# One expert per tile of sorted tokens instead of all experts for every token

## The reference, cut to what matters

```
gate_logits = jnp.einsum('bpd,de->bpe', x, W_gate)
top_w, top_idx = jax.lax.top_k(gate_logits, K)            # K = 2 of E = 8
top_w = jax.nn.softmax(top_w, axis=-1)
...
for e in range(E):
    h = jax.nn.gelu(jnp.einsum('bpd,dm->bpm', x, W_in[e]) + b_in[e], approximate=False)
    y = jnp.einsum('bpm,md->bpd', h, W_out[e]) + b_out[e]
    out = out + combine[..., e, None] * y                 # combine is 0 for 6 of 8 experts
```

## Time and profile before

| | |
|---|---|
| median of 3 runs | 4415.43 us |
| the profiled execution, its own time | 4414.62 us |
| its span in the trace | 4412.8 us |
| busy share of the span | PE 94%, DVE 83%, ACT 74%, POOL 41% |
| expert phase, from its first instruction to the end | 3872.3 to 4412.8 us |

### The profile page before, as it was taken

How to read it: one execution, slowest core, us unless ns; L and a number is a source line. 1 busy time by engine, 2 the same in 40 slices (tenths; PEclk the granted TensorE clock), 3 DMA queues, 4 the chain that set the end, 5 groups by cost and what they waited for, 6 DMA issues and landing times. The chain is left out here.

```text
span 4412.8 us, 116370 instructions
## 1 busy us (share of the span) xinstructions
PE 4161.9 (94%) x43493; PEld 3278.8 (74%) x43493; DVE 3681.6 (83%) x6452; ACT 3261.0 (74%) x5155; POOL 1825.8 (41%) x983
## 2 busy tenths in 40 slices
PE   6887689999999999999999999999999999879999
PEld 2434268888888888888888888888888888757776
DVE  7889688888888888888888888888888888657776
ACT  5888567777777777777777777777777777546666
POOL 0000255555555555555555555555555555200000
PEclk9999799999999999999999999999999999979999
DMA  2111132322332323323233222333223222211110
GB/s 84 44 44 44 35 71 67 70 67 66 88 73 65 71 62 89 74 63 71 62 92 71 67 67 63 96 67 70 63 64 98 65 69 68 50 63 45 48 43 29
DMA packets 351688, 287.85 MB, mean 65 GB/s; under 512 B 231920, under 2 KB 236400, under 8 KB 350000
## 3 DMA queue, kind: packets, MB, share of 16 engines
q1 hardware_dynamic: 351152, 280.60, 26.1%
HBM read 45.45 MB, written 4.33 MB: 11 GB/s over the span
## 5 line engine op out<-in xcount | busy, mean ns | idle before, releaser
L702 POOL TENSOR_TENSOR qk_rotated<-qk_rotated,rotary_sines 128x1024 f32<-128x1024 f32 x384 | 924.3, 2407 | 1414.4 <-DVE rotary_sines L783 1414.4
L713 POOL TENSOR_TENSOR qk_rotated<-qk_rotated,rnorm 128x1024 f32<-128x1024 f32 x384 | 733.2, 1910 | 7.4
L791 DVE TENSOR_REDUCE qk_sumsq<-qk_squared 128x16 f32<-128x1024 f32 x384 | 465.3, 1212 | 97.5 <-ACT qk_squared L525 97.5
L232 PE MATMUL ps_proj<-qkv_w_hi,x_shifted_hi 128*128 128x512 f32 x1152 | 511.6, 444 | 15.9 <-DVE rotary_sines L783 11.7
L532 ACT ACTIVATE q_t<-ps_qk_t 128x512 f32<-128x512 f32 x384 | 229.5, 598 | 401.6 <-PE ps_qk_t L288 392.3
L773 DVE TENSOR_TENSOR qk_rotated<-ps_proj,rotary_scaled 128x1024 f32<-128x1024 f32 x384 | 467.2, 1217 | 7.6 <-ACT qk_squared L525 7.6
L783 DVE TENSOR_TENSOR rotary_sines<-ps_proj,rotary_scaled 128x1024 f32<-128x1024 f32 x384 | 466.3, 1214 | 1.7 <-POOL qk_rotated L702 1.7
L234 PE MATMUL ps_proj<-qkv_w_hi,x_shifted_lo 128*128 128x512 f32 x1152 | 459.6, 399 | 0.0
L546 ACT ACTIVATE k_t_by_head<-ps_qk_t 64x512 f32<-64x512 f32 x768 | 451.2, 587 | 11.0 <-PE ps_qk_t L297 1.6
L233 PE MATMUL ps_proj<-qkv_w_lo,x_shifted_hi 128*128 128x512 f32 x1152 | 456.1, 396 | 0.0
L313 PE MATMUL ps_scores<-k_t_by_head,q_t 128*32 128x128 f32 x12288 | 415.1, 276 | 9.8 <-ACT ps_scores L555 5.1
(11 more groups left out here) (304 smaller groups left out, 9694.7 us busy)
## 6 DMA issues: line engine op xcount, KB each, us to landing
v_by_window<-v_tokens SPq DMA_DIRECT2D x1152, 128.0 KB, 2.4
v_by_window<-v_tokens SPq DMA_DIRECT2D x384, 64.0 KB, 2.1
k_t_by_head<-k_t_by_head SPq DMA_DIRECT2D x96, 256.0 KB, 4.4
e_w_in<-combine_saved SPq DMA_DIRECT2D x64, 256.0 KB, 3.0
v_by_window<-v_by_window SPq DMA_DIRECT2D x192, 64.0 KB, 2.0
qkv_w_raw<-in_layer_qk_dram SPq DMA_DIRECT2D x7, 1664.0 KB, 8.8
f_k_stacked<-f_k_hi SPq DMA_DIRECT2D x64, 64.0 KB, 2.0
f_k_stacked<-f_k_lo SPq DMA_DIRECT2D x64, 64.0 KB, 2.0
```

The source lines that it names most:

```text
L232: mm(out, hi, HI[:, o:o + 512], start=True, stop=False)
L702: tt(u, u, TB[:], ALU.add).then_inc(added, 1)
L713: tt(u, u, r.unsqueeze(3).broadcast_to((P, 2, 8, DH)), ALU.mult).then_inc(scaled, 1)
L791: nc.vector.reduce_sum(SS[:, 16 * i:16 * i + 16], SQ[:].rearrange("p (h e) -> p h e", e=DH), AX).then_inc(sumsq, 1)
```

## The change

The dense loop over blocks and experts is replaced. First, for all 8 blocks: the sum x1, its layer norm, the normed rows turned to token order (`XR`, 130 words a row: 128 features, a destination and a weight) and back, the gate, and the top 2 of 8. A scan over all one-hot choices and two matmuls rank the 8192 choices by expert; each expert's run of slots is rounded up to a multiple of 512, so that there are at most 23 tiles (TILES) of 512 slots, and each tile has one expert. POOL then issues 64 indirect row transfers of 128 rows into a DRAM array `expert_rows`, which SP has filled with empty slots before (6.1 MB). Beside that runs the attention of all blocks, in an order of its own for each engine, and leaves the stream in `XF` (`base`). SP, ACT and POOL also split each expert's weights into high and low parts and store them in DRAM (1 MB an expert).

Then the tiles run, always 23. For tile t, SP loads 512 rows (266 KB, four buffers) and, by a register that it loads from `EID`, the bias and the split weights of the tile's expert (0.5 MB for each of the two matrices, two buffers). PE turns the rows, computes four hidden and four output quarters (each three split matmuls) and turns the result back; DVE weighs it; POOL writes its 512 rows to DRAM (`expert_y`) with four indirect transfers, by the destinations that came with the rows. At the end SP loads the two results of each token, DVE adds them to the stream, and SP stores it.

In the features phase the semaphores are cleared and given back at the end, with one more barrier, so that there are enough of them.

```diff
@@ features_phase @@
-            return ctx.enter_context(nc.semaphore("f_" + name))
+            signals.append(nc.alloc_semaphore(name="f_" + name))
+            return signals[-1]
...
+    nc.clear_and_free_semaphores(signals)
+    nc.all_engine_barrier()
...
@@ constants @@
+TILES = (TOPK * B * N + E_ * (BLK - 1)) // BLK
+NSLOT = TILES * BLK
+ROWW = P + 2
-HS_ = 3
+EHALF = 2 * HM * P
...
@@ experts_phase: sync @@
-            sp.dma_start(WI[:], w_in).then_inc(experts_in, 16)
-            sp.dma_start(WO[:], w_out).then_inc(experts_in, 16)
...
+            sp.dma_start(XN[:, 1:4, :], x_attn[:, 1:4, :]).then_inc(xa_in[0], 16)
+            sp.dma_start(XN[:, 4:NBLK, :], x_attn[:, 4:NBLK, :]).then_inc(xa_in[1], 16)
+            sp.dma_start(xs, slots).then_inc(filled, 16)
+            for e in range(2):
+                sp.dma_start(WR[e][:], expert_w[e]).then_inc(w_in[e], 16)
+            for e in range(E_):
+                sp.wait_ge(w_high, e + 1)
+                sp.wait_ge(w_low, e + 1)
+                sp.dma_start(split[e], WB[e % 2][:].rearrange("p s x -> p (s x)").bitcast(F32)).then_inc(w_saved[e % 2], 16)
+                if e + 2 < E_:
+                    sp.dma_start(WR[e % 2][:], expert_w[e + 2]).then_inc(w_in[e % 2], 16)
+            for k in range(2):
+                sp.wait_ge(w_saved[k], 16 * E_ // 2)
+            sp.wait_ge(expert_ids, 1)
+
+            def load_rows(t):
+
+                if t >= 4:
+                    sp.wait_ge(y_saved[t % 2], 16 * NT * ((t - 4) // 2 + 1))
+                if t >= 2:
+                    sp.wait_ge(x_hi, t - 1)
+                sp.dma_start(XT[t % 4][:].rearrange("p c d -> p (c d)"),
+                             xs[t * BLK:(t + 1) * BLK, :].rearrange("(p c) d -> p (c d)", c=NT)).then_inc(xt_in[t % 2], 16)
+
+            def load_weights(t):
+
+                e = sp.value_load(EID[0:1, t:t + 1], min_val=0, max_val=E_ - 1)
+                if t >= 2:
+                    sp.wait_ge(h_out, HM * (t - 1))
+                sp.dma_start(EB[t % 4][:], expert_b[e]).then_inc(wi_in[t % 2], 16)
+                sp.dma_start(WB[t % 2][:, 0, :].bitcast(F32), split[e, :, 0:EHALF]).then_inc(wi_in[t % 2], 16)
+                if t >= 2:
+                    sp.wait_ge(y_out, t - 1)
+                sp.dma_start(WB[t % 2][:, 1, :].bitcast(F32), split[e, :, EHALF:2 * EHALF]).then_inc(wo_in[t % 2], 16)
+            load_weights(0)
+            sp.wait_ge(scattered, 16 * NPOS)
+            load_rows(0)
+            for t in range(TILES):
+                if t + 1 < TILES:
+                    load_rows(t + 1)
+                if t > 0:
+                    load_weights(t)
+            for k in range(2):
+                sp.wait_ge(y_saved[k], 16 * NT * ((TILES + 1 - k) // 2))
+            for k in range(4):
+                w = 2 * NT * TOPK * P
+                sp.dma_start(YL[:, 2 * k:2 * k + 2].rearrange("p i c s d -> p (i c s d)"), ytok[:, k * w:(k + 1) * w]).then_inc(y_in[k], 16)
+            for i in range(NBLK):
+                sp.wait_ge(summed, i + 1)
+                sp.dma_start(out[:, i], tokens(XF2(XF, i))).then_inc(x_out, 16)
...
@@ experts_phase: tensor @@
+            def ranks():
+                pe.wait_ge(counted, 1)
+                mm(TOTAL[:, 0:E_], ONES[:], INC[:, :, NPOS - 1], start=True, stop=True).then_inc(rank_mm, 1)
+                pe.wait_ge(counted, 2)
+                pe.wait_ge(zc_out, NBLK)
+                mm(RANK[:], TRI[:], OH[:].rearrange("p e k -> p (e k)"), start=True, stop=False)
+                mm(RANK[:], ONES[:], EX[:].rearrange("p e k -> p (e k)"), start=False, stop=True).then_inc(rank_mm, 1)
...
+            def rows_in(t):
+                pe.wait_ge(xt_in[t % 2], 16 * (t // 2 + 1))
+                after(pe, x_hi, t)
+                after(pe, x_lo, t)
+                pe.wait_ge(base, NBLK)
+                for c in range(NT):
+                    last = flip(XP[:, chunk(c)], XT[t % 4][:, c, 0:P], IDENT[:])
+                last.then_inc(xp_mm, 1)
+
+            def hidden(t, m):
+                b = t % 2
+                if m == 0:
+                    pe.wait_ge(wi_in[b], 32 * (t // 2 + 1))
+                    pe.wait_ge(x_hi, t + 1)
+                after(pe, h_out, HM * (t - 1) + m + 1)
+                if t == 0:
+                    pe.wait_ge(hs_out, NBLK)
+                mm(HB[m][:], WB[b][:, 0, chunk(m)], XHI[b][:], start=True, stop=False)
+                mm(HB[m][:], WB[b][:, 0, chunk(HM + m)], XHI[b][:], start=False, stop=False)
+                if m == 0:
+                    pe.wait_ge(x_lo, t + 1)
+                mm(HB[m][:], WB[b][:, 0, chunk(m)], XLO[b][:], start=False, stop=True).then_inc(h_mm, 1)
+
+            def output(t, m):
+                b = t % 2
+                if m == 0:
+                    pe.wait_ge(wo_in[b], 16 * (t // 2 + 1))
+                    after(pe, y_out, t - 1)
+                pe.wait_ge(h_lo, HM * t + m + 1)
+                mm(YB[b][:], WB[b][:, 1, chunk(m)], HHI[:, b, m, :], start=(m == 0), stop=False)
+                mm(YB[b][:], WB[b][:, 1, chunk(m)], HLO[:, b, m, :], start=False, stop=False)
+                last = mm(YB[b][:], WB[b][:, 1, chunk(HM + m)], HHI[:, b, m, :], start=False, stop=(m == HM - 1))
+                if m == HM - 1:
+                    last.then_inc(y_mm, 1)
+
+            def rows_out(t):
+                pe.wait_ge(y_out, t + 1)
+                after(pe, yo_out, t)
+                for c in range(NT):
+                    last = flip(YT[:, chunk(c)], YS[t % 2][:, chunk(c)], IDENT[:])
+                last.then_inc(yt_mm, 1)
+            rows_in(0)
+            for t in range(TILES + 2):
+                for m in range(HM):
+                    if t < TILES:
+                        hidden(t, m)
+                    if 0 <= t - 1 < TILES:
+                        output(t - 1, m)
+                    if m == 1 and t + 1 < TILES:
+                        rows_in(t + 1)
+                    if m == 2 and t >= 2:
+                        rows_out(t - 2)
...
@@ experts_phase: scalar @@
+            def weights_high(e):
+                b = e % 2
+                act.wait_ge(w_in[b], 16 * (e // 2 + 1))
+                after(act, w_saved[b], 16 * (e // 2))
+                a(WB[b][:, :, 0:HM * P], halves(WR[b][:]), ACT.Copy).then_inc(w_high, 1)
...
+            for i in range(NBLK):
+                act.wait_ge(centered, i + 1)
+                after(act, var_mm, i - 1)
+                a(ZQ[i % 2][:], G[i % 2][:], ACT.Square).then_inc(sq, 1)
+                a(XN[:, i, :], G[i % 2][:], ACT.Copy).then_inc(zc_out, 1)
+                if i >= 6:
+                    weights_high(i - 6)
...
+            for t in range(TILES):
+                for m in range(HM):
+                    act.wait_ge(h_mm, HM * t + m + 1)
+                    after(act, h_lo, HM * (t - 1) + m + 1)
+                    a(H[:, m, :], HB[m][:], ACT.Gelu, bias=EB[t % 4][:, m:m + 1]).then_inc(h_out, 1)
+                    if m > 0:
+                        hidden_high(t, m - 1)
+                    elif t > 0:
+                        hidden_high(t - 1, HM - 1)
+                    if m == 2 and t + 1 < TILES:
+                        rows_high(t + 1)
...
@@ experts_phase: gpsimd (all of it new) @@
+            def weights_low(e):
+                b = e % 2
+                pool.wait_ge(w_high, e + 1)
+                after(pool, w_saved[b], 16 * (e // 2))
+                nc.gpsimd.tensor_tensor(WB[b][:, :, HM * P:2 * HM * P], halves(WR[b][:]),
+                                        WB[b][:, :, 0:HM * P].bitcast(F32), ALU.subtract).then_inc(w_low, 1)
+            pool.wait_ge(payload, 1)
+            pool.wait_ge(weights, 2)
+            pool.wait_ge(rows1, NBLK)
+            pool.wait_ge(placed, 1)
+            for k in range(NPOS):
+                s, g = k // NG, k % NG
+                nc.gpsimd.indirect_dma_start(out=xs, out_offset=bass.IndirectOffsetOnAxis(ap=POSI[:, k:k + 1], axis=0),
+                                             in_=XR[:, s, g, :], in_offset=None).then_inc(scattered, 16)
+                if k % 8 == 4 and k // 8 + 2 < E_:
+                    weights_low(k // 8 + 2)
+            for t in range(TILES):
+                pool.wait_ge(yo_out, t + 1)
+                for c in range(NT):
+                    nc.gpsimd.indirect_dma_start(
+                        out=yout, out_offset=bass.IndirectOffsetOnAxis(ap=XT[t % 4][:, c, P:P + 1].bitcast(U32), axis=0),
+                        in_=YO[t % 2][:, c, :], in_offset=None).then_inc(y_saved[t % 2], 16)
...
@@ experts_phase: vector @@
+            def output(t):
+                dve.wait_ge(y_mm, t + 1)
+                after(dve, yt_mm, t - 1)
+                ts(YS[t % 2][:], YB[t % 2][:], EB[t % 4][:, HM:HM + 1], None, ALU.add).then_inc(y_out, 1)
+
+            def weighed(t):
+                dve.wait_ge(yt_mm, t + 1)
+                after(dve, y_saved[t % 2], 16 * NT * (t // 2))
```

(72 more changed lines are left out.)

912 lines of the change are left out of this document (411 added, 501 removed).

## The result

| | before | the change |
|---|---|---|
| median | 4414.3 us (4 runs) | 4552.1 us (4 runs, 4551.4 to 4564.5) |
| ratio | 1 | 1.032, 95% interval 1.030 to 1.034 |
| profiled execution | 4414.6 us, span 4412.8 | 4552.1 us, span 4550.3 |
| expert phase | 541 us | 679 us, from 3871.4 |
| tile loop (before: the PE-bound part) | 470 us, PE busy 462 | 476 us, first hidden matmul to the landing of the last scatter |

A forecast was written before the change was run, and what follows sets the result against it. PE was taken to bound the kernel before, a chain of waits the tile loop after. 3871.9 + 1.5 handover + 190 start + 513 loop + 19 end + 1.8 outside the span gave 4597 us, range 4470 to 4780.

The forecast's parts named there:

- the handover: Barrier after the features phase: cleared semaphores add between 0 and another handover of 2.2 us; taken as 1.5.
- start to the first hidden matmul: Expert phase before the tile loop: 190 us, with 77 to `placed`, then attention beside POOL's scatter; ends 165 and 235.
- loop: Tile loop: 513 us, from filling, 22 turns mostly of 24.5 us, and 25 to drain.
- end: After the tile loop: four loads of 1 MB, DVE steps for the last two blocks and a store, 19 us.
- Some 420 us of waiting: Whole change: 210 us of PE work are taken out and some 420 us of waiting put in.
- The mechanism of the loop: Tile loop: a tile's weights stand on SP behind rows waiting for `y_saved` of an earlier tile, so PE waits.
- the faster rival: Tile loop: the scatter gives no wait and PE sets the turn, 179 us instead of 513, 4263 us; chance 0.05.
- The size of the turn: Tile loop, from one tile's first hidden matmul to the next's: legs sum to 24.3 us, taken as 24.5.
- the landing: Tile loop, scatter of results to DRAM: lands 2.0 us after the issue, as today's 256 KB store.
- the rival that POOL is dear: POOL's indirect transfers: 2.4 us each, scatter opens the loop, turn 29.3 us, total 4755 us; chance 0.17.
- The clock: PE's leg of a turn: 12 matmuls at 0.43 us after standing, 9 at 0.23, 1.2 of transposes: 8.4 us.
- Attention, not the scatter, opens the tile loop: Start of the expert phase: attention path ends at 190 us, POOL's transfers and splits beside it at 170.

The follow-up runs named there:

- rows: The change with eight row buffers in place of four, so a row load waits for outputs of seven tiles before: 4292.3 us, 0.972 of before.
- order: The change with SP issuing the weights of tile t ahead of the rows of tile t+1: 4452.8 us, 1.009 of before.
- weighing: The change with the transposes of a tile's results and their weighing moved to the second slot of the tile loop: 4479.6 us in one run.
- the early one: The change with SP's register load of the expert's number moved ahead of the wait for the saved outputs: 4560.4 us in one run.
- PE kept busy: The change with 15 unused full-precision matmuls of 128x512 added at the end of each tile on PE: 4524.4 us in one run.

## Why the prediction was right, point by point

The sum by its own terms: phase from 3871.4 (forecast 3873.4, with 1.5 for the handover), start to the first hidden matmul 183.2 (190), loop 476.3 (513), end 19.4 (19), and 1.8 outside the span: 4552.1. Of the error of 45 us, 37 lie in the loop and 7 in the start. ("Some 420 us of waiting" is 393 by the forecast's own numbers, 183 more in all and 210 taken out; by the measured time it is 348.) The handover between the phases grew by 0.7 us, to 3.2 (the earlier trace rows has 2.53; SP's timeline of the change):

```profile
519.11 0.32 SPq L1063 DMA_DIRECT2D x_attn<-f_y  x1
522.34 0.34 SPq L155 DMA_DIRECT2D rotary<-in_rotary_dram  x1
```

*The mechanism of the loop* was right. Three edits that take the wait or a leg out of the chain (rows, order, weighing) shorten the turn as the chain says, the order by 1 to 2 us less than expected, and with the wait gone PE sets the turn, as the faster rival would have it. That rival was given 4263 us; the kernel made for it took 4246. The Trainium skill ("DMA: Bandwidth & Descriptors", section Rules for kernel authors) says that an early issue and a late wait hide a transfer's fixed cost. The kernel with eight row and three weight buffers agrees (5.1 us to landing, PE busy for 97% of the loop), and the change shows the other side, where the issue itself waits.

*The size of the turn* was 1.8 us too large, and 18 turns of that are 32 of the 37 us by which the loop was over. The mis-sized terms are the landing ("2.0 after the issue") and SP ("2.5"). The scatter landed 2.25 us after its issue began, as the store in the earlier trace rows, but POOL's instruction is 0.97 of that, so 1.3 was left, not 2.0. On SP the register load, which no row had shown and which was put at 1.0, costs 0.57 (what the early one took off the leg), and the whole leg is 1.61.

*POOL* was taken at 1.2 us a transfer, as the middle of 0.63 and 2.41. It is 0.97 and 0.30 between two:

```profile
L2094 POOL DMA_INDIRECT expert_y<-e_q,e_tile_rows x92: 963/969/1436, 4076.7 to 4528.6; - x92
```

(nanoseconds: least, median, most). That ends the rival that POOL is dear. That 1.2 lies so near 1.27 is partly luck, since neither of the two rows was of an indirect transfer.

The Trainium skill ("SBUF — State Buffer", section A bandwidth-pool intuition that's wrong (but worth ruling out), not the section that the prediction names) gives about 620 ns for a transfer issued from GpSimd alone and about 3100 ns beside a VectorE copy, because it waits until VectorE releases a shared port. The trace agrees with a wait for VectorE's instruction, but not with that size: none of 156 transfers took over 1.50 us, with DVE busy for 74 of the 114 us from 3940 to 4054 beside the 64 of the sorting. Of these 64, 13 took over 1.00 us, and 11 of the 13 began while DVE was at `e_q`, `e_k` or `e_k_min`, steps that read and write SBUF alone, and ended 0.83 to 0.86 us behind the end of that step. One of them:

```profile
3996.64 0.69 DVE L2242 TENSOR_TENSOR e_q<-e_q,e_q_exp 128x512 f32<-128x512 f32 x1 [0.22 <-DVE e_ksum_heads L2235]
3996.73 1.44 POOL L2086 DMA_INDIRECT expert_rows<-e_rows,e_place_index  x1 [0.30 <-issue]
```

So the wait is short because these steps are, at most 0.69 us; that the port is its cause was not tested.

*The clock* was chosen at 12 matmuls at 0.43 and 9 at 0.23: 8.4 forecast, 8.14 measured, 6.01 with PE kept busy (6.0 was the bound). This term alone is 2.1 us a turn. The level came from rows, the count of 12 from none: in the change 5 to 11 distances a turn are 0.43, 8.6 in the mean, and that the sum came so near is partly luck.

*The start* came out near (183 for 190, and POOL's first transfer 73.8 us in, for 77), but one reason in it was wrong. "ScalarE (ACT) stands at `weights_high(0)`" for the fill "about 30 us": it stood 2.72 us. The fill took 26.6 us and was over about when ACT arrived, because PE comes to the next block's two-pass matmul only every 3.4 us, at a granted clock of 0.51 from 3874 to 3900 us:

```profile
3890.72 2.05 PE L1806 MATMUL e_ps<-stream,e_centering 128*128 128x512 f32 x2
3894.14 2.06 PE L1806 MATMUL e_ps<-stream,e_centering 128*128 128x512 f32 x2
```

```profile
3900.03 1.06 ACT L1995 ACTIVATE e_w_split<-e_w_raw 128x1024 fp32r<-128x1024 f32 x1 [2.72 <-DMA e_w_raw<-in_expert_w_dram]
```

Eight blocks by 3.4 us take as long as the fill; the right number came from the wrong one of the two. "Attention, not the scatter, opens the tile loop" held, though the scatter's splits delay attention.

## What to carry to other kernels

When a change trades busy time for transfers, write down for each queue what stands behind each wait, and follow the buffer whose release that wait needs: here a row buffer was held by its last word's use, three tiles later, and the next weights stood behind it on SP. A chain through all engines is found by adding its legs and checked by moving one leg at a time; the largest gain here came not from a faster leg (4.0 us a turn at most) but from enough buffers to take the wait off the chain (16 us a turn, 4552 to 4246 us, with four more row buffers and one more weight buffer). A queue that holds two kinds of work, as POOL's transfers and splits, couples the chains that each serves, so before one wait is removed, ask which chain ends next.

## What the runs showed of the hardware that was not expected

- A row load of 260 KB delays the half megabyte of weights close behind it: weights issued 1.6 us behind the rows landed in 4.05 us, issued 1.0 us behind them in 5.01, so the earlier issue lost time.
- Behind a pause of 2.69 us PE's next matmuls started 0.43 us apart (eight row buffers, 4157.65 on: six of them, then 0.23); behind the pauses of 0.47 to 0.76 us that the added matmuls left, 0.23 from the second on.
- An indirect transfer of 128 rows costs POOL 1.27 us whether its rows are 520 bytes (the sorting) or 512 (the results).
- An indirect transfer that POOL begins beside a DVE step within SBUF ends 0.83 to 0.86 us behind that step (11 of 64 in the sorting). The other way round, a DVE step of 128x32 on the way to `placed` (L2143, 0.18 us alone) that began beside POOL's weight split from 3901.17 to 3905.83 us took 2.11 us, until 3905.87; with the fill behind the weights it took 0.64, until 0.04 us behind the end of a split.
